# The causal mask of the row scores moves from a product on TensorE into VectorE's maximum

## The reference

```
att = jnp.einsum('bhqd,bhkd->bhqk', q, k) / math.sqrt(HEAD_DIM)
causal = jnp.triu(jnp.ones((s, s), dtype=bool), k=1)
att = jnp.where(causal[None, None, :, :], jnp.float32(-1000000000.0), att)
att = jax.nn.softmax(att, axis=-1)
out = jnp.einsum('bhqk,bhkd->bhqd', att, v)
```

## Time and profile before

| | |
|---|---|
| device time, three runs | 3356.23, 3358.98, 3374.25 us; median 3358.98 |
| profiled execution, first to last instruction | 3356.4 us |
| TensorE busy | 3138.2 us, 93% |
| VectorE busy | 2074.8 us, 62% |
| ScalarE busy | 1589.8 us, 47% |
| attention stage | about 172 to 819 us of the span |

### The profile page before, as it was taken

The page is one execution under the profiler, slowest core; times in us unless marked ns, Lnnn a source line. Parts: engine busy times, 40 slices in busy tenths (PEclk is TensorE's granted clock), DMA queues, the critical chain, the costliest instruction groups (busy, mean ns, idle before and its releaser), DMA issues. The chain is left out here.

```text
span 3356.4 us, 62801 instructions
## 1 busy us (share of the span) xinstructions
PE 3138.2 (93%) x15964; PEld 2447.5 (73%) x15965; DVE 2074.8 (62%) x3588; ACT 1589.8 (47%) x2095; POOL 885.0 (26%) x768
## 2 busy tenths in 40 slices
PE   7979999999899899999999968878998999999996
PEld 6745555555577699999999933336777999999995
DVE  4256666663585466666666649988654666666664
ACT  2224444444321256665665656634124665565663
POOL 0011000010011233334343314430122444343432
PEclk9969999999999999999999979989998999999998
DMA  5331111130310367777777540124016777777765
GB/s 175 114 76 40 40 40 39 40 99 4 114 37 23 110 174 167 174 175 167 182 180 173 109 131 0 50 72 159 21 42 173 180 174 178 175 172 175 168 139 111
DMA packets 141339, 383.49 MB, mean 114 GB/s; under 512 B 22112, under 2 KB 22880, under 8 KB 137568
## 3 DMA queue, kind: packets, MB, share of 16 engines
q1 hardware_dynamic: 87456, 252.66, 24.1%
q0 software_dynamic: 52608, 127.69, 20.1%
q10 hardware_dynamic: 1152, 1.57, 0.2%
HBM read 281.42 MB, written 104.63 MB: 115 GB/s over the span
## 5 line engine op out<-in xcount | busy, mean ns | idle before, releaser
L1727 DVE TENSOR_TENSOR first_lo<-first_raw,first_hi x232 | 562.8, 2426 | 118.9 <-ACT first_hi L1670 118.4
L1624 POOL DMA_INDIRECT acc_rows<-g_y,first_ids_out x232 | 377.6, 1628 | 896.3 <-ACT g_y L1681 698.3
L594 DVE TENSOR_REDUCE b_part_max<-b_p_ring 128x1 f32<-128x512 f32 (+3 forms) x640 | 360.1, 606 | 230.9 <-PE b_p_ring L681 143.4
L1670 ACT ACTIVATE first_hi<-first_raw x232 | 469.5, 2024 | 49.9 <-DMA first_raw<-in_expert_weights_dram 30.9
L568 ACT ACTIVATE b_probs<-b_p_cols 128x1024 f32<-128x1024 f32 (+1 forms) x320 | 269.2, 893 | 322.5 <-PE b_p_cols L699 322.5
L1720 DVE TENSOR_TENSOR g_hidden<-g_gate,g_p_up 128x352 f32<-128x352 f32 x232 | 120.9, 521 | 449.2 <-PE g_p_up L1787 444.8
L1785 PE MATMUL g_p_gate<-first_hi,g_rows_hi 128*128 x928 | 321.6, 347 | 6.7 <-DVE first_lo L1727 6.4
L1681 ACT ACTIVATE g_y<-g_p_y,first_rows_in 128x512 f32<-128x512 f32 x232 | 159.4, 687 | 331.0 <-PE g_p_y L1803 331.0
L1786 PE MATMUL g_p_gate<-first_lo,g_rows_hi 128*128 x928 | 302.6, 326 | 0.0
L1787 PE MATMUL g_p_gate<-first_hi,g_rows_lo 128*128 x928 | 301.5, 325 | 0.0
L1786 PE MATMUL g_p_up<-first_lo,g_rows_hi 128*128 x928 | 298.6, 322 | 0.0
(11 more groups left out here) (327 smaller groups left out, 6435.1 us busy)
## 6 DMA issues: line engine op xcount, KB each, us to landing
first_raw<-in_expert_weights_dram SPq DMA_DIRECT2D x248, 544.0 KB
acc_rows<-f_acc SPq DMA_DIRECT2D x34, 256.0 KB, 2.0
qk_hi<-a_hi SPq DMA_DIRECT2D x32, 256.0 KB, 2.6
qk_lo<-a_lo SPq DMA_DIRECT2D x32, 256.0 KB, 2.9
xn_rows<-f_xn SPq DMA_DIRECT2D x8, 1024.0 KB, 10.5
b_q_stack<-qk_hi SPq DMA_DIRECT2D x28, 256.0 KB
b_k_stack<-qk_hi SPq DMA_DIRECT2D x28, 256.0 KB
first_raw<-in_expert_weights_dram SPq DMA_DIRECT2D x2, 2176.0 KB, 9.4
```

The source lines that it names most:

```text
L594: v.tensor_reduce(part_max[:, h, t % BT, c:c + 1], p_ring[:, ring, 0:w], AX.X, ALU.max).then_inc(rows_free, 1)
L1624: pool.indirect_dma_start(out=acc_rows, out_offset=bass.IndirectOffsetOnAxis(ap=ids_out[:, i:i + 1].bitcast(U32), axis=0), in_=y[:, n, :], ...
L1670: act.activation(hi[:, bass.ds(place, PIECE)], raw[:, bass.ds(source, PIECE)], ACT.Copy).then_inc(split_hi_ready, 1)
L1727: v.tensor_tensor(lo[:, bass.ds(place, PIECE)], raw[:, bass.ds(source, PIECE)], hi[:, bass.ds(place, PIECE)].bitcast(F32), ALU.subtract).t ...
```

## The change

The mask product on TensorE is gone, and each masked unit is one matmul. VectorE takes the maximum of a masked unit by `tensor_tensor_reduce`: it reads the bank and a mask from SBUF, adds them, writes the sum as bf16 to a scratch tile that nothing reads, and gives the maximum of the sum. The mask is now 128 x 512 in fp32, zero but for its last 128 columns, and a unit w wide reads its last w columns. A semaphore increment (`max_order`) stands ahead of it. Other units keep their plain maximum. GpSimd makes one constant fewer.

```diff
@@ constants @@
-        mask = sb("b_mask", [P, P], BF16)
-        ident_b = sb("b_ident", [P, P], BF16)
-        zeros_b = sb("b_zeros", [P, P], BF16)
+        mask = sb("b_mask", [P, BW])
+        masked_rows = sb("b_masked_rows", [P, NRING, BW], BF16)
...
@@ GpSimd @@
-                chain.link(pool.memset(zeros_b[:], 0.0))
-                pool.affine_select(out=ident_b[:], in_=zeros_b[:], compare_op=ALU.not_equal, fill=1.0,
-                                   base=0, pattern=[[-1, P]], channel_multiplier=1).then_inc(rows_const, 1)
-                pool.affine_select(out=mask[:], in_=zeros_b[:], compare_op=ALU.is_ge, fill=MASKED,
+                chain.link(pool.memset(mask[:], 0.0))
+                pool.affine_select(out=mask[:, BW - P:BW], in_=mask[:, BW - P:BW], compare_op=ALU.is_ge, fill=MASKED,
...
@@ VectorE, reduce_unit @@
-                    v.tensor_reduce(part_max[:, h, t % BT, c:c + 1], p_ring[:, ring, 0:w], AX.X, ALU.max).then_inc(rows_free, 1)
+                    if c * BW + w == (t + 1) * P:
+                        v.sem_inc(max_order, 1)
+                        v.tensor_tensor_reduce(masked_rows[:, ring, 0:w], p_ring[:, ring, 0:w], mask[:, BW - w:BW], 1.0, LOWEST,
+                                               ALU.add, ALU.max, part_max[:, h, t % BT, c:c + 1]).then_inc(rows_free, 1)
+                    else:
+                        v.tensor_reduce(part_max[:, h, t % BT, c:c + 1], p_ring[:, ring, 0:w], AX.X, ALU.max).then_inc(rows_free, 1)
...
@@ TensorE, rows_unit @@
-                diagonal = c * BW + w == (t + 1) * P
-                mm = pe.matmul(p_ring[:, ring, 0:w], q_stack[i][h][0:NPART, t * P:(t + 1) * P],
-                               k_stack[i][h][0:NPART, c * BW:c * BW + w], start=True, stop=not diagonal)
-                if diagonal:
-                    mm = pe.matmul(p_ring[:, ring, w - P:w], ident_b[:], mask[:], start=False, stop=True)
-                mm.then_inc(rows_ready, 1)
+                pe.matmul(p_ring[:, ring, 0:w], q_stack[i][h][0:NPART, t * P:(t + 1) * P],
+                          k_stack[i][h][0:NPART, c * BW:c * BW + w], start=True, stop=True).then_inc(rows_ready, 1)
```

More of the change, by code:

```diff
@@ L400, in stage_attention @@
         const, rows_const = k.sem("b_const_ready"), k.sem("b_rows_const_ready")
-        N_CONST, N_ROWS_CONST = 2, 3
+        N_CONST, N_ROWS_CONST = 2, 2
         loaded = [k.sem(f"b_stack_loaded{i}") for i in range(2)]
         v_ready = k.sem("b_v_ready")
-        masked, mask_order = k.sem("b_masked"), k.sem("b_mask_order")
+        masked, mask_order, max_order = k.sem("b_masked"), k.sem("b_mask_order"), k.sem("b_max_order")
         stack_free, shift_moved = k.sem("b_stack_free"), k.sem("b_shift_moved")
```

## The result

The changed kernel takes 3333.63 us (median of 5 runs, 3328.34 to 3342.88) against 3359.10 of the kernel before beside it (5 runs): a ratio of 0.992, 95% interval 0.989 to 0.994. It is 25 us faster, and I forecast 13.8, with a range whose lower end was 3335. Two later sets of runs of the same kernel gave 3340.13 and 3339.20, ratios of 0.995 (0.994 to 0.997) and 0.994 (0.992 to 0.996). The unchanged stages scatter by nearly as much as the gain: from the attention stage's last value product to the end of the span takes 2532 to 2550 us in the traces of this study, whatever the kernel. "The steady part" is the time from the start of its first value product to the start of its last: 599.5 us before and 575.2 after.

What follows compares the result with a forecast made beforehand. TensorE was taken as the bound, busy 76.44 of 77 us in a steady stretch. The gain 19.6 - 1.5 - 2.5 - 0.7 - 1.1 = 13.8 us turned 3358.98 into 3345.2 us, with an 8-in-10 range of 3335 to 3359.

Steps and rivals of the forecast that it cites:

- What goes: Mask products on TensorE in the steady part: 88 pairs at 0.19 us and 29 at 0.10, 19.6 us gained.
- The cheaper mask: Skill's matmul rule, 56 ns a mask: 234 steady masks worth 13.1 us, net gain near 8; the trace was preferred.
- VectorE's surplus per pair: Two fused maxima with their result writes take 1.67 us against 1.29 for two plain ones: 0.38 us more.
- Place A: Once per head pair, VectorE gapless from masked pair through shift to four maxima: 2.5 us lost, 1.5 of masks not gained.
- Place B: Seven times, a unit soon after a masked 384-wide pair needs its bank: 0.1 of 0.19 us lost, 0.7 in all.
- The fill: Start of the attention stage: three masked pairs where VectorE runs without a gap, 3 x 0.38 = 1.1 us lost.
- hidden everywhere: Rival: VectorE's added time never reaches TensorE, as second instruction overlaps next main one; gain 19.6 us, 3339.4; chance 0.16.
- The rival of VectorE as the pace: Main fused instruction runs at the scan's 1315 ns, so the kernel is slower by 20 us, 3379; chance 0.09.
- the nearly free masks: Rival: two masks cost TensorE only 0.08 us a pair, 0.04 at 128 wide; gain 3.6 us, 3355.4; chance 0.12.

Runs made afterwards that it cites:

- e3: The kernel before with its loop over head pairs written out on every engine, so no branch back: 3348.67 us, ratio 0.998.
- e4: The changed kernel with its loop over head pairs written out in the same way: 3331.68 us, ratio 0.993.
- e6: The kernel before with the row scores' mask left out on both engines: no mask products, plain maxima everywhere; 3336.70 us.
- e5: The kernel before, unchanged, traced once more: 3365.85 us in one execution.

## Why the forecast was too small

The step that failed is one that the sum doesn't have: it put TensorE's branch back at nothing, and in the first pair of traces the branch is worth 6.9 us. The rest of the shortfall is in sizes. The stage ended 25.2 us earlier in the span than before. It consists of 17.4 for the change in the steady part (e3 against e4), 6.9 for the branch back, and 0.9 ahead of the first value product (0.4 of it ahead of the stage's first row product). My sum had 13.8. The steps of the sum:

1. *What goes: right.* Forecast 12 x 0.19 + 4 x 0.10 = 2.7 us for a head pair. From e3 to e6 the passages of the sixteen masked pairs of one head pair shorten by 0.19 to 0.21 us each at 256 and 512 columns, by 0.17 to 0.19 at 384 and by 0.07 to 0.14 at 128, 2.7 in all. The cheaper mask that I set beside it by the Trainium skill's rule for a matmul (13.1 us) is refuted for this place.
2. *VectorE's surplus per pair: the mis-sized term.* I took 0.38 us; on VectorE it is 0.02 at 512 columns and 0.13 at 128. The 83 ns instead of 145 is the smaller part. The greater is that I put main instruction and read end to end and compared that with two plain maxima that overlap. Against that, I gave nothing to the added semaphore increment, and a fused pair starts later: 0.60 us behind its first product (611.91 to 612.51), where an unmasked plain one takes 0.43. Between busy instructions it starts 0.15 us behind the maximum ahead of it, where plain ones follow without a gap. The increment stands in that gap; that it makes it isn't shown by a run.
3. *Place A: direction right, size nearly.* I forecast that it moves by 0.31 us the wrong way, 2.5 in all, and that 1.5 of its masks is not gained. Measured between the starts of the row pairs m = 0 and m = 3 on TensorE, in the five head pairs that are neither the first nor just behind a branch, it takes 4.48 to 4.50 us before, 4.42 to 4.44 with TensorE's half alone (e6: 0.07 of the masks' 0.19 is gained, as forecast), and 4.58 to 4.84 after, 0.24 more than before on average. Unrolled it is 4.57, so 0.09 more (e4 against e3). TensorE's wait isn't where I looked for it. The wait of the row pair stays as it was; a new one stands in front of the turning of the shift, which the late fused pair delays. Before, and after, in the last head pair:
```profile
757.13 0.30 PE L689 MATMUL b_p_ring<-ident,b_shift 128*128 128x128 f32 x1
757.64 1.10 PE L681 MATMUL b_p_ring<-b_k_stack,b_q_stack 96*128 96x512 f32 x2 [0.21 <-DVE b_part_max L594]
```
```profile
730.56 0.69 DVE L593 CUSTOM_DVE_ANT_0 b_masked_rows<-b_p_ring,b_mask 128x512 bf16<-128x512 f32 x1 [0.16 <-PE b_p_ring L682]
...
732.64 0.30 PE L687 MATMUL b_p_ring<-ident,b_shift 128*128 128x128 f32 x1 [0.17 <-DVE b_shift L607]
733.15 1.10 PE L682 MATMUL b_p_ring<-b_k_stack,b_q_stack 96*128 96x512 f32 x2 [0.21 <-DVE b_part_max L596]
```
In three of the five head pairs another 0.25 us comes to it, because the last small step of the shift starts 0.44 us behind the one ahead of it and not 0.21. This is so in the looped kernels with the fused form and never in an unrolled one; its cause is open.
4. *Place B: forecast 0.1 of 0.19 lost each time; right.* From the masked pair to the products it took 1.74 us (596.25 to 597.99) and takes 1.69, so 0.14 is lost.
5. *The fill: forecast 1.1 lost.* From the eight maxima to TensorE's next row product it takes 4.81 us before and after, with the same wait:
```profile
205.58 2.48 DVE L596 TENSOR_REDUCE b_part_max<-b_p_ring 128x1 f32<-128x512 f32 x4 [0.20 <-PE b_p_ring L682]
...
210.39 1.19 PE L682 MATMUL b_p_ring<-b_k_stack,b_q_stack 96*128 96x512 f32 x2 [1.00 <-DVE b_part_max L596]
```
6. *Together* these steps gave 14.9 us for the steady part; it is 17.4. Seven head pairs at 2.7 (e6 against e3) and the last at 58.89 - 58.17 = 0.7 make 19.6 for TensorE's half, if the undisturbed head pairs stand for all; with what A and B keep of the masks my sum had 17.9. So 1.7 us are TensorE's, and no row shows where they are made good. VectorE's surplus is the difference, 19.6 - 17.4 = 2.2, where I had 8 x 0.38 = 3.0. With the 1.1 of the fill this is 3.6 of the missing 11.4.
7. *The step that was not there: the branch back.* I counted what an instruction costs while it runs and nothing for its place in the loop's code. The two idle times "<-issue" of 2.0 and 1.7 us and the windows at 0.50 stood in the trace of before, and I read a stretch that had neither. In this trace they are 6.9 us, more than the errors of the other steps together; against e5 they are 4.3. With them, the change's own rows would have given 19.6 - 2.2 + 6.9 = 24.3.

So the masks' price and the direction of A and B were right, the surplus was too large by the overlap, and the greatest part of what the forecast missed in the stage came from a step that it didn't have. That the median of all runs, 3338.7, lies near the 3339.4 of the rival "hidden everywhere" is luck: the surplus isn't hidden everywhere, and the branch is in that time. The overlap that this rival wanted is there, the absence of a cost is not. The rival of VectorE as the pace is refuted by 689 ns, and the nearly free masks by the 2.7 us.

## What to carry to other kernels

Before a change that adds or removes instructions in a loop, look at the loop's edge: an idle time "<-issue" of a microsecond or more behind the branch back was here the sign of a body too long or badly placed, and then an instruction has a price beside its duration. Measure the body in instructions, matmul and weight load counted apart, and shorten, shift or unroll it. Price an engine's added instruction by the distance between starts, not by the sum of durations, where the instructions it replaces overlap; look for its cost at the next thing that waits for the engine, which here was the turning of the shift; and read the windows of a whole stage, not of its quietest part, before saying where its time goes. Let the traced stage decide where the whole program scatters by as much as the gain.

## What the runs showed of the hardware

- A body of 1665 records branches back in 0.21 to 0.23 us or in 3.3 us, by its position alone; 1793 and 1805 take 3.3 to 3.8. TensorE is idle for less than that: 1.6 to 2.4 us behind 14 of the 15 long branches, 3.5 us behind one of 4.7. Even with short branches the looped kernel's steady part is 1.3 to 1.6 us longer than the unrolled one's.
- Behind such an idle time the granted clock is at 0.50 for 3.4 to 10.2 us in 13 of 15 cases and not at all in two (e5's first branch, with 1.63 us of idle time, and before's second, with 1.74). In e6 it fell behind idle times of 0.78 and 0.31 us.
- The add-and-maximum of a PSUM and an SBUF operand runs at the pace of the plain maximum at 512 columns, and its result is read in 83 ns, mostly within the record of the main instruction. With the semaphore increment ahead of it, it starts 0.60 us behind its product, against 0.43 of an unmasked plain maximum.
